# Reordering the hand-written instruction orders of a Mamba layer with a mixture of experts, five engines on one core

## The reference

```python
xz = layernorm(x) @ W_in + b_in                 # 128 -> 2 * 256
u, z = silu(xz[:, :256]), xz[:, 256:]
B, C = split(u @ W_xproj + b_xproj)             # 16 states each
dt = softplus(u @ W_dt + b_dt)
h_t = exp(dt_t * A) * h_{t-1} + dt_t * u_t * B_t   # per channel and state
y_t = sum_s h_t[s] * C_t[s] + D * u_t
x = x + (y * silu(z)) @ W_out + b_out
n = layernorm(x)
p = softmax(n @ gate_w.T); comb = p where among the top 2 of p + gate_bias, else 0
x = x + shared(n) + sum_e comb[:, e] * expert_e(n)   # 8 experts of width 256
# expert(n) = (silu(n @ w1.T) * (n @ w3.T)) @ w2.T
```

## Time and profile before

| | |
|---|---|
| median of 3 runs | 1292.01 us (1288.14 to 1292.46) |
| profiled execution, its own time | 1290.66 us |
| its span | 1288.5 us |
| busy PE / DVE / ACT / POOL | 1179.8 / 1174.2 / 1126.6 / 1112.8 us |
| TensorE clock granted, mean | 0.97 of full speed |
| DMA | 152.74 MB, 31.3% of 16 engines' time |

### The profile page before, as it was taken

One profiled execution on the slowest core, in us unless ns is written; L12 is line 12 of the kernel. 1 busy time (PEld: TensorE's weight loads), 2 busy tenths in 40 slices (PEclk: granted clock), 3 DMA queues, 4 the chain that ended last, 5 costly groups with the idle time before them and its releaser, 6 DMA issues.

```text
span 1288.5 us, 25674 instructions
## 1 busy us (share of the span) xinstructions
PE 1179.8 (92%) x7200; PEld 946.2 (73%) x7200; DVE 1174.2 (91%) x1833; ACT 1126.6 (87%) x1965; POOL 1112.8 (86%) x902
## 2 busy tenths in 40 slices
PE   4565899999999999999999999999999999999998
PEld 2334587877878787787778777777878778788887
DVE  1779899999999999999999999999999999999954
ACT  6674889999998999999899999989989998999854
POOL 2999899898999989899998989999898999998700
PEclk8776899999999999999999999999999999999999
DMA  8233331605234160523415052331505243250000
GB/s 305 121 146 125 133 148 39 250 1 207 82 132 155 54 232 0 205 81 137 150 62 225 0 205 81 144 142 67 220 0 210 77 152 135 71 208 9 10 9 9
DMA packets 47942, 152.74 MB, mean 119 GB/s; under 512 B 4512, under 2 KB 29472, under 8 KB 31392
## 3 DMA queue, kind: packets, MB, share of 16 engines
q1 hardware_dynamic: 47904, 152.28, 31.3%
HBM read 147.03 MB, written 5.24 MB: 118 GB/s over the span
## 4 chain that ended last, share of the span: by engine, by line
POOL 27%; issue 23%; PE 22%; DVE 19%; ACT 7%; DVEq 1%; DMA 0%; POOLq 0%; ACTq 0%; SPq 0%
POOL dbu L673 16%; PE h L938 10%; POOL hc L681 7%; DVE da L773 6%; PE mixed L907 5%; DVE hc L773 5%; PE y_acc L920 4%; POOL dt_s L661 3%; DVE g L815 2%; ACT L625 2%; ACT silu L625 2%; ACT da L589 1%; DVE acc L823 1%; DVE stats L743 1%; DVE hc L781 1%
## 5 line engine op out<-in xcount | busy, mean ns | idle before, releaser
L673 POOL TENSOR_TENSOR dbu<-w_s,b_all 128x512 f32<-128x512 f32 x512 | 650.3, 1289 | 5.7 <-DVE da L773 3.0
L681 POOL TENSOR_TENSOR hc<-hc,c_all 128x512 f32<-128x512 f32 x272 | 350.5, 1292 | 82.1 <-DVE hc L773 80.6
L589 ACT ACTIVATE da<-dt_s,a_neg 128x512 f32<-128x512 f32 x512 | 346.7, 692 | 84.2 <-DVE hc L781 70.0
L773 DVE TENSOR_TENSOR_SCAN hc<-da,dbu 128x512 f32<-128x512 f32 x272 | 328.1, 1211 | 12.0 <-PE y_acc L920 10.9
L920 PE MATMUL y_acc<-ident,hc 128*128 128x128 f32 x2048 | 295.0, 280 | 32.5 <-POOL hc L681 27.3
L773 DVE TENSOR_TENSOR_SCAN da<-da,dbu 128x512 f32<-128x512 f32 x240 | 292.6, 1219 | 27.4 <-ACT da L589 15.1
L920 PEld LDWEIGHTS y_acc<-ident,hc 128*128 128x128 f32 x2048 | 247.5, 144 | 81.5 <-POOL hc L681 36.2
L907 PE MATMUL mixed<-w_s,g 128*128 128x128 f32 x2304 | 283.4, 276 | 3.2 <-DVE g L815 1.2
L907 PEld LDWEIGHTS mixed<-w_s,g 128*128 128x128 f32 x2304 | 270.6, 192 | 15.4 <-DVE g L815 10.1
L938 PE MATMUL h<-x_hi,w_hi 128*128 128x512 f32 x576 | 264.1, 458 | 7.4 <-DVE g L815 2.9
L938 PE MATMUL h<-x_hi,w_lo 128*128 128x512 f32 x576 | 228.4, 396 | 0.0
(11 more groups left out here) (77 smaller groups left out, 1063.6 us busy)
## 6 DMA issues: line engine op xcount, KB each, us to landing
b_all<-bc_rows SPq DMA_DIRECT2D x64, 1024.0 KB, 4.7
c_all<-bc_rows SPq DMA_DIRECT2D x64, 1024.0 KB, 6.8
xt<-in_x SPq DMA_DIRECT2D x16, 256.0 KB, 6.5
res<-in_x SPq DMA_DIRECT2D x16, 256.0 KB, 6.9
out<-acc SPq DMA_DIRECT2D x16, 256.0 KB, 2.3
silu<-in_w SPq DMA_DIRECT2D x6, 256.0 KB, 4.1
w_s<-in_w SPq DMA_DIRECT2D x1, 1152.0 KB, 6.9
bc_rows<-bc_rows_s SPq DMA_DIRECT2D x16, 64.0 KB, 1.6
```

What stands on the lines that cost most here:

```text
L589: act.activation(da[a % DA_SLOTS][:, :], dt_s[:, c, :], ACT.Exp, scale=a_neg[:, a:a + 1]).then_inc(decay_made, 1)
L673: pool.tensor_tensor(dbu[:, a % DBU_SLOTS, :], w_s[:, c, :], b_all[:, s, :], ALU.mult).then_inc(dbu_made, 1)
L681: pool.tensor_tensor(slot, slot, c_all[:, s, :], ALU.mult).then_inc(c_by_pool, 1)
L773: dve.tensor_tensor_scan(dst, ring[:, :], dbu[:, a % DBU_SLOTS, :], 0.0, ALU.mult, ALU.add).then_inc(scanned, 1)
```

## The change

Only the three texts of orders and the code that reads them are changed; each engine has the same tasks as before, with the same shapes, buffers and semaphores. `START_ORDER` now covers sequences 0 to 2, `ORDER` windows 3 to 13 (4 to 13 as the loop), `END_ORDER` the last two windows. `LEAD` is 2, `LAG` 3. The window is cut elsewhere: PE's begins with `red.20` of sequence n-1 instead of `red.0` of n.

```diff
@@ -42,124 +42,205 @@
 ORDER = {
     "pe": """
-        red.0 red.1 red.2 h1.11-2 h3.9-2 gy.1-1 h1.12-2 red.3 eo.4-2 red.4 proj.0-1 h3.10-2 red.5 h1.13-2
-        z.0 z.1 h1.14-2 h1.15-2 h3.11-2 red.6 red.7 h3.12-2 red.8 eo.5-2 red.9 h3.13-2 x_t.0+1 red.10
-        h1.16-2 h1.17-2 xp.0+1 xp.1+1 h3.14-2 red.11 eo.6-2 red.12 h3.15-2 red.13 dl.0+1 h3.16-2 red.14
-        red.15 bc.0+1 h3.17-2 split.0-1 red.16 red.17 eo.7-2 red.18 dl.1+1 red.19 red.20 h1.0-1 red.21
-        red.22 h1.1-1 h1.2-1 eo.8-2 h3.0-1 h3.1-1 route.0-1 h3.2-1 red.23 red.24 h1.3-1 red.25 red.26 h1.4-1
-        eo.0-1 red.27 h1.5-1 gy.0 h1.6-1 h3.3-1 h3.4-1 eo.1-1 h3.5-1 h1.7-1 h3.6-1 red.28 h1.8-1 red.29
-        eo.2-1 h3.7-1 h3.8-1 red.30 red.31 eo.3-1 h1.9-1 h1.10-1
+        red.20-1 eo.5-3 red.21-1 dl.0 dl.1 red.22-1 red.23-1 red.24-1 red.25-1 h3.13-3 h3.14-3 eo.6-3
+        h3.15-3 split.0-2 h3.16-3 red.26-1 h1.17-3 red.27-1 h3.17-3 red.28-1 red.29-1 eo.7-3 red.30-1 h1.0-2
+        h1.1-2 h3.0-2 red.31-1 route.0-2 eo.8-3 h3.1-2 h1.2-2 red.0 h1.3-2 h1.4-2 red.1 red.2 h1.5-2 h1.6-2
+        red.3 h3.2-2 red.4 h1.7-2 h1.8-2 gy.1-1 h3.3-2 eo.0-2 h3.4-2 red.5 red.6 eo.1-2 proj.0-1 h3.5-2
+        red.7 h1.9-2 red.8 h1.10-2 h1.11-2 z.0 h3.6-2 eo.2-2 red.9 z.1 red.10 h1.12-2 red.11 h3.7-2 h1.13-2
+        red.12 h3.8-2 h3.9-2 x_t.0+1 eo.3-2 red.13 red.14 red.15 eo.4-2 h3.10-2 h1.14-2 h1.15-2 red.16
+        red.17 xp.0+1 xp.1+1 h1.16-2 red.18 gy.0 h3.11-2 bc.0+1 red.19 h3.12-2
     """,
     "act": """
-        zs.0 zs.1 silu.14-2 silu.15-2 decay.11 decay.12 norm1.0+1 decay.13 sc.5-2 x_tc.0+1 decay.14 decay.15
-        silu.16-2 u.0+1 silu.17-2 u.1+1 decay.16 decay.17 sc.6-2 norm2.0-1 decay.18 decay.19 dlc.0+1 ycopy.0
-        bcc.0+1 decay.20 splitc.0-1 xhi.0-1 decay.21 skip.0+1 decay.22 sc.7-2 decay.23 dlc.1+1 decay.24
-        decay.25 silu.0-1 silu.1-1 silu.2-1 decay.26 decay.27 sc.8-2 softe.0+1 rexp.0-1 decay.28 decay.29
-        softl.0+1 silu.3-1 silu.4-1 silu.5-1 silu.6-1 decay.30 decay.31 sc.1-1 decay.0+1 decay.1+1 silu.7-1
-        silu.8-1 decay.2+1 sc.2-1 decay.3+1 ycopy.1 decay.4+1 sc.3-1 decay.5+1 silu.9-1 silu.10-1 silu.11-1
-        decay.6+1 decay.7+1 decay.8+1 sc.4-1 decay.9+1 decay.10+1 silu.12-1 silu.13-1
+        norm1.0 decay.10-1 decay.11-1 sc.1-3 decay.12-1 silu.9-3 silu.10-3 silu.11-3 zs.0-1 decay.13-1
+        sc.2-3 decay.14-1 decay.15-1 silu.12-3 silu.13-3 zs.1-1 decay.16-1 decay.17-1 x_tc.0 sc.3-3
+        decay.18-1 decay.19-1 ycopy.0-1 sc.4-3 decay.20-1 decay.21-1 u.0 silu.14-3 u.1 silu.15-3 silu.16-3
+        decay.22-1 decay.23-1 norm2.0-2 decay.24-1 bcc.0 sc.5-3 decay.25-1 decay.26-1 dlc.0 decay.27-1 dlc.1
+        softe.0 decay.28-1 decay.29-1 softl.0 decay.30-1 decay.31-1 sc.6-3 splitc.0-2 xhi.0-2 decay.0
+        decay.1 silu.17-3 sc.7-3 silu.0-2 silu.1-2 decay.2 rexp.0-2 decay.3 ycopy.1-1 skip.0 sc.8-3 decay.4
+        decay.5 silu.2-2 silu.3-2 silu.4-2 silu.5-2 silu.6-2 decay.6 decay.7 silu.7-2 silu.8-2 decay.8
+        decay.9
     """,
     "dve": """
-        gyc.1-1 scan.6 mul.6 scan.7 scan.8 mul.8 comb.4-2 projc.0-1 mom1.0+1 g.10-2 agg1.0+1 scan.9 scan.10
-        g.11-2 mul.10 nb1.0+1 g.12-2 scan.11 scan.12 mul.12 scan.13 comb.5-2 mom2.0-1 agg2.0-1 g.13-2
-        scan.14 mul.14 scan.15 nb2.0-1 g.14-2 scan.16 scan.17 mul.16 comb.6-2 scan.18 g.15-2 mul.18 scan.19
-        scan.20 xlo.0-1 mul.20 scan.21 scan.22 mul.22 scan.23 g.16-2 g.17-2 comb.7-2 scan.24 mul.24 scan.25
-        g.0-1 scan.26 routec.0-1 mul.26 scan.27 rank.0-1 g.1-1 rank.1-1 comb.8-2 rank.2-1 g.2-1 rank.3-1
-        rank.4-1 scan.28 rank.5-1 rank.6-1 mul.28 scan.29 comb.0-1 g.3-1 gyc.0 g.4-1 rank.7-1 scan.30
-        scan.31 g.5-1 scan.0+1 comb.1-1 mul.0+1 g.6-1 scan.1+1 g.7-1 scan.2+1 mul.2+1 scan.3+1 comb.2-1
-        g.8-1 scan.4+1 scan.5+1 comb.3-1 mul.4+1 g.9-1
+        scan.7-1 gyc.1-2 g.3-3 comb.0-3 scan.8-1 mul.8-1 scan.9-1 scan.10-1 mul.10-1 g.4-3 g.5-3 comb.1-3
+        projc.0-2 scan.11-1 scan.12-1 mom2.0-2 mul.12-1 g.6-3 scan.13-1 comb.2-3 scan.14-1 g.7-3 scan.15-1
+        mul.14-1 agg2.0-2 g.8-3 scan.16-1 g.9-3 mul.16-1 scan.17-1 scan.18-1 mul.18-1 scan.19-1 comb.3-3
+        comb.4-3 g.10-3 scan.20-1 mul.20-1 nb2.0-2 scan.21-1 gyc.0-1 g.11-3 scan.22-1 mul.22-1 scan.23-1
+        scan.24-1 mul.24-1 comb.5-3 scan.25-1 scan.26-1 g.12-3 mul.26-1 scan.27-1 g.13-3 scan.28-1 mom1.0+1
+        scan.29-1 mul.28-1 g.14-3 g.15-3 scan.30-1 scan.31-1 comb.6-3 g.16-3 scan.0 xlo.0-2 mul.0 g.17-3
+        agg1.0+1 scan.1 comb.7-3 routec.0-2 g.0-2 scan.2 rank.0-2 mul.2 rank.1-2 scan.3 g.1-2 comb.8-3
+        rank.2-2 scan.4 rank.3-2 mul.4 rank.4-2 nb1.0+1 rank.5-2 scan.5 rank.6-2 g.2-2 scan.6 rank.7-2 mul.6
     """,
     "pool": """
-        hcp.7 dbu.10 dbu.11 rs1.0+1 dbu.12 dbu.13 hcp.9 hcp.11 dbu.14 dbu.15 hcp.13 dbu.16 rs2.0-1 dbu.17
-        dbu.18 dbu.19 hcp.15 dbu.20 hcp.17 dbu.21 dbu.22 dbu.23 hcp.19 dbu.24 hcp.21 dbu.25 dbu.26 hcp.23
-        hcp.25 dbu.27 dbu.28 dbu.29 hcp.27 dbu.30 dt.0+1 dbu.31 w.0+1 hcp.29 dbu.0+1 hcp.30 hcp.31 dbu.1+1
-        dbu.2+1 dbu.3+1 dt.1+1 dbu.4+1 dbu.5+1 hcp.1+1 dbu.6+1 hcp.3+1 dbu.7+1 hcp.5+1 dbu.8+1 resb.0
-        dbu.9+1 w.1+1
+        dbu.0-1 hcp.30-2 dbu.1-1 hcp.31-2 dbu.2-1 dbu.3-1 dbu.4-1 hcp.1-1 hcp.3-1 rs1.0 dbu.5-1 dt.1-1
+        dbu.6-1 dbu.7-1 dbu.8-1 hcp.5-1 dbu.9-1 dbu.10-1 dbu.11-1 hcp.7-1 hcp.9-1 resb.0-2 dbu.12-1 dbu.13-1
+        dbu.14-1 w.1-1 hcp.11-1 dbu.15-1 dbu.16-1 hcp.13-1 dbu.17-1 dbu.18-1 hcp.15-1 dbu.19-1 dbu.20-1
+        dbu.21-1 hcp.17-1 rs2.0-2 dbu.22-1 dbu.23-1 hcp.19-1 dbu.24-1 hcp.21-1 dbu.25-1 dbu.26-1 hcp.23-1
+        dbu.27-1 dbu.28-1 hcp.25-1 dbu.29-1 dbu.30-1 hcp.27-1 dbu.31-1 dt.0 w.0 hcp.29-1
     """,
     "sp": """
-        load.0+1 rows.0+1 spread.0+1 spread.1+1 store.0-2 spread.2+1 spread.3+1 loadres.0
+        loadres.0-1 rows.0+1 load.0+2 spread.0+1 spread.1+1 spread.2+1 store.0-2 spread.3+1
     """,
 }
 
 START_ORDER = {
     "pe": """
-        x_t.0 xp.0 xp.1 bc.0 dl.0 dl.1 z.0 red.0 red.1 red.2 red.3 z.1 x_t.0+1 red.4 red.5 red.6 xp.0+1
...
+        x_t.0 xp.0 xp.1 z.0 bc.0 dl.0 dl.1 z.1 red.0 red.1 x_t.0+1 red.2 red.3 red.4 xp.0+1 red.5 red.6
+        xp.1+1 red.7 red.8 dl.0+1 red.9 red.10 red.11 bc.0+1 red.12 red.13 dl.1+1 red.14 red.15 red.16
+        red.17 red.18 red.19 red.20 red.21 red.22 red.23 red.24 gy.0 red.25 red.26 red.27 red.28 red.29
+        red.30 red.31 red.0+1 gy.1 red.1+1 proj.0 z.0+1 red.2+1 red.3+1 red.4+1 red.5+1 red.6+1 z.1+1
+        red.7+1 x_t.0+2 red.8+1 red.9+1 xp.0+2 red.10+1 xp.1+2 red.11+1 red.12+1 red.13+1 red.14+1 red.15+1
+        bc.0+2 gy.0+1 dl.0+2 red.16+1 red.17+1 red.18+1 dl.1+2 red.19+1 split.0 red.20+1 route.0 red.21+1
...
     """,
     "act": """
-        norm1.0 x_tc.0 u.0 u.1 bcc.0 whi.0 dlc.0 dlc.1 softe.0 softl.0 decay.0 zs.0 decay.1 norm1.0+1 skip.0
...
+        norm1.0 x_tc.0 u.0 u.1 zs.0 bcc.0 dlc.0 dlc.1 softe.0 softl.0 decay.0 decay.1 skip.0 whi.0 whi.1
+        zs.1 decay.2 whi.2 decay.3 norm1.0+1 decay.4 decay.5 decay.6 x_tc.0+1 decay.7 decay.8 decay.9
...
     """,
     "dve": """
-        mom1.0 agg1.0 nb1.0 mom1.0+1 agg1.0+1 nb1.0+1 scan.0 mul.0 scan.1 scan.2 scan.3 mul.2 scan.4 wlo.0
...
+        mom1.0 agg1.0 nb1.0 mom1.0+1 agg1.0+1 scan.0 mul.0 scan.1 scan.2 nb1.0+1 scan.3 mul.2 scan.4 mul.4
+        scan.5 scan.6 scan.7 mul.6 scan.8 mul.8 scan.9 scan.10 mul.10 wlo.0 wlo.1 mom1.0+2 scan.11 scan.12
+        mul.12 scan.13 scan.14 scan.15 wlo.2 mul.14 scan.16 agg1.0+2 mul.16 scan.17 scan.18 mul.18 scan.19
+        scan.20 mul.20 scan.21 scan.22 scan.23 mul.22 wlo.3 scan.24 wlo.4 wlo.5 mul.24 scan.25 scan.26
+        mul.26 scan.27 scan.28 mul.28 scan.29 gyc.0 scan.30 scan.31 wlo.6 scan.0+1 scan.1+1 mul.0+1 scan.2+1
+        nb1.0+2 mul.2+1 scan.3+1 scan.4+1 gyc.1 mul.4+1 scan.5+1 scan.6+1 mul.6+1 scan.7+1 projc.0 wlo.7
+        mom2.0 scan.8+1 mul.8+1 scan.9+1 agg2.0 scan.10+1 scan.11+1 wlo.8 mul.10+1 scan.12+1 scan.13+1
+        mul.12+1 scan.14+1 mul.14+1 nb2.0 scan.15+1 scan.16+1 mul.16+1 scan.17+1 scan.18+1 mul.18+1 gyc.0+1
+        scan.19+1 scan.20+1 mul.20+1 scan.21+1 scan.22+1 mul.22+1 scan.23+1 scan.24+1 mul.24+1 xlo.0
...
     """,
     "pool": """
-        rs1.0 resb.0 rs1.0+1 dt.0 dt.1 w.0 w.1 dbu.0 dbu.1 dbu.2 dbu.3 dbu.4 dbu.5 hcp.1 hcp.3 dbu.6 dbu.7
...
+        rs1.0 rs1.0+1 resb.0 dt.0 dt.1 w.0 w.1 dbu.0 dbu.1 dbu.2 dbu.3 dbu.4 hcp.1 dbu.5 dbu.6 hcp.3 dbu.7
...
     """,
     "sp": """
-        load.0 loadres.0 rows.0 load.0+1 spread.0 spread.1 spread.2 spread.3 rows.0+1 spread.0+1 spread.1+1
-        spread.2+1 spread.3+1
+        load.0 load.0+1 loadres.0 rows.0 spread.0 spread.1 spread.2 load.0+2 spread.3 rows.0+1 spread.0+1
+        spread.1+1 spread.2+1 spread.3+1 load.0+3 rows.0+2 spread.0+2 spread.1+2 spread.2+2 spread.3+2
+        loadres.0+1 rows.0+3 load.0+4 spread.0+3 spread.1+3 spread.2+3 spread.3+3 store.0
     """,
 }
 END_ORDER = {
     "pe": """
...
+        eo.5-4 red.20-2 red.21-2 dl.0-1 dl.1-1 red.22-2 red.23-2 red.24-2 h3.13-4 red.25-2 h3.14-4 h3.15-4
```

(58 more changed lines are left out.)

141 lines of the change are left out of this document (94 added, 47 removed).

## The result

The changed kernel takes **1312.11 us** (median of 4 runs, 1305.33 to 1321.28) where the kernel before, run beside it, took 1291.03 (1288.14 to 1292.46): a ratio of 1.017, 95% interval 1.010 to 1.025. It is slower, where 1283 was forecast, and outside the range. The profiled execution is the longest of the four (1321.28 us), so its rows show more of the trouble than the median has.

A forecast was written before the change was run, and what follows sets the result against it. No single engine was taken as the bound: four lie within 3.3 us per window, and order decides the brief waits. 1290.66 + 0.5 - 4.5 - 3.3 - 9 + 8.6 = 1283 us; range 1268 to 1303.

The forecast's parts named there:

- Costs used: All engines: fixed start-to-start costs per instruction, summed per window to DVE 71.1, PE 67.7, ACT 67.9, POOL 69.3 us before.
- The window: Repeated window, sequences 3 to 12: 73.9 us instead of 74.8 from more even orders, -9 us over ten windows.
- evenness over stretches of eight steps: Repeated window: average of the largest engine sum per eight-step stretch falls from 76.1 to 75.2 us; 1.2% taken as gain.
- Table loads: ACT: 14 per window instead of 13, 226 in all instead of 209; 1.28 us more per window, covered by idle time.
- Then it costs nothing: ACT's extra 1.28 us table load per window is free while ACT keeps its present 5.2 us of idle time.
- The start: Up to sequence 2: first `dt` chain about 1 us later, counted +0.5; sequence 1 -4.5 us, sequence 2 -3.3 us.
- the -3.3: Sequence 2: 71.5 us instead of 74.8, with sums DVE 63.1, PE 62.2, ACT 62.3, POOL 69.3.
- The end: Sequences 13 to 15 and after: FFN work comes back, +0.5, +4.7, +0.9 and +2.5, together +8.6 us.
- Tail: FFN behind the last `red`: PE has 60.4 us for 57.9, so +2.5 on 63.0 us.
- The slower one: Rival, chance 0.22: in each window `res` reloads too late and POOL's `resb` waits; 1307 us.
- The tight window: Rival, chance 0.18: the window tightens to DVE's busy time, 72.7 us, -21 instead of -9; 1271 us.
- nothing comes of it: Rival, chance 0.18: buffers already absorb uneven stretches, so evenness gives nothing; edges leave +1.3, 1292 us.

The follow-up runs named there:

- experiment 1: Changed kernel with `var + eps` written as a sum by tensor_reduce instead of tensor_scalar: 1296.14 us, ratio 1.0045.
- experiment 2: Kernel before with `var + eps` written as a sum by tensor_reduce instead of tensor_scalar: 1280.32 us, ratio 0.992.
- second edit: The ranking's all-pairs comparison reads one operand from PSUM, on top of tensor_reduce for `var + eps`: 1276.00 us in the old order, 1301.59 in the new.
- experiments 11 and 8: `var + eps` by tensor_reduce and one operand of the ranking's comparison from PSUM: 11 in the changed kernel, 1301.59 us; 8 in the kernel before, 1276.00 us.
- experiment 3: Kernel before with `softl` two decays earlier in the repeated window, one more table load per window: 1294.22 us, ratio 1.0025.
- Experiment 6: Kernel before with tensor_reduce for `var + eps` and six of each sequence's 36 `h1` and `h3` computed twice on PE: 1339.99 us, ratio 1.038.
- lock-free: Either kernel with `var + eps` by tensor_reduce instead of tensor_scalar: changed kernel 1296.14 us, kernel before 1280.32 us.
- Experiments 9 and 10: Kernel before with tensor_reduce for `var + eps` and 10.5 us of PE work doubled: 9 in the start, 1285.33 us; 10 at the end, 1290.51 us.

## Why the prediction was wrong, by its steps

Forecast and profiled span differ by 38.7 us (-7.7 and +31.0): 31.4 of them in the ten windows (-9 and +22.4), 3.7 up to sequence 2, 3.6 in the end. Of the windows' +22.4 the lock on `var + eps` makes 25.1, less the 6.8 that it cost the same windows before, and the new order +4.2.

The whole span splits in the same way: experiment 1 minus experiment 2 is the order without this lock, 1294.1 - 1278.4 = +15.7 us; the lock costs the changed kernel 1319.5 - 1294.1 = 25.4 and the kernel before 1288.5 - 1278.4 = 10.1. Together 15.7 + 25.4 - 10.1 = 31.0. In medians 15.8 + 16.0 - 10.6 = 21.2. The +15.7 is not the order's cost free of all locks: with the second edit in both kernels (experiments 11 and 8) the spans are 1301.6 and 1276.7, 24.9 apart.

**Costs used: failed.** I took each instruction to have one duration and made sums of an order from them. `var + eps` was in none of the rows I read; in my sums it was a trifle. Its time depends on where it stands beside POOL's text, so a new order changes a cost and not only waits. By the spans that is 15 us, half of the profiled difference; by the medians 5, a quarter.

**The window: failed.** 73.9 was forecast; 75.1 is the best and 77.1 the mean of the ten. Without the lock it is 74.5 against 74.1 of the old order: evenness over stretches of eight steps gained nothing, although the sums fell by 1.2%. DVE is busy for 1.1 us less there (70.74 for 71.88 us), but now it waits for ACT, in the window from 547.87 of experiment 1 (total us, times, longest):

```profile
DVE da L870 <- ACT da L682: 2.6, 3, 1.4
```

Before, that was 0.3. Each of the three scans waits for a `decay` that stands right behind a table load (at 556.16, 579.86 and 594.37), and none of these loads is the new one behind `softl` (at 609.80). So the 0.23 us per window of experiment 3, 2.3 of the ten windows' +4.2, can't simply be carried over; no run tested where the loads stand in the new order. This step was the bulk of the forecast, and nothing of before had shown that evenness over such stretches is worth anything.

**Table loads: count right, price wrong.** "Then it costs nothing" was 0.23 us per window in the old order. An engine's idle time, summed over a window, covers a load only where that idle time lies. The Trainium skill (ScalarE: Activation LUTs, "Table sets: the hidden batching unit") has exp and ln in one set. The trace doesn't agree: a load of 1.28 us stands between `softl` and the next `decay` in the new order too (at 609.80 in experiment 1), and 17 more loads were run in all.

**The start: half right.** The first `dt` comes at 26.96 for 26.40, as forecast. From `hcp.31` of sequence 0 to that of 1 it is 70.4 us for 70.5 forecast, but the first of them ends 3.1 us later than before (102.02 for 98.93), so by this mark only 1.5 us are gained up to the end of sequence 1; the copies of `y_acc` have +1.0 and 68.4 for 73.8. Sequence 2 has 75.5, 73.9 without the lock, for 71.5: the -3.3 did not come. It is nearly as full as any other window (PE 68.7, DVE 69.9, ACT 67.8, POOL 70.4 us busy of 73.9), only with a largest sum of 69.3, and I let the largest sum stand for the time. Experiment 6 shows what that misses.

**The end: mechanism right, size wrong**, +12.2 for +8.6 (lock-free +15.1). The two stretches that carry it, sequence 13 and 14 of experiment 1:

```profile
994.71:1073.94 79.23, 76.45 (x470) 60.90 (x470) 76.75 (x121) 75.03 (x134) 71.80 (x60) 1.00 0.32 121
1073.94:1155.85 81.91, 81.35 (x519) 68.04 (x518) 76.53 (x116) 77.11 (x135) 68.47 (x55) 1.00 0.29 105
```

Against 74.1 each in experiment 2 that is +5.1 and +7.8 for forecasts of +0.5 and +4.7. In sequence 13 PE is busy for 4.7 us more than in experiment 2 (71.74) and the time grows by 5.1; I had let PE's 72.5 vanish under a window of 74.8 that it did not set. DVE and ACT are busy for 4.9 and 5.6 us more there, so that it is PE that sets this time is not shown; in sequence 14, where PE is busy for 81.35 of 81.91 us, it is. Tail: +1.9 for +2.5, right. PE's busy time moved is 10.7 + 3.1 us out of sequences 1 and 2, and 4.7 + 9.6 + 0.1 + 2.0 into the end. Experiments 9 and 10 give these 47% and 97%: about -6.5 and +16; measured -4.7 (-3.5 with the later start chain) and +15.1. That this comes so near is in part luck: the start's price is loose, and the change moved DVE and ACT work along with PE's.

**Rivals.** The slower one had the right sign and nearly the size (1307), by the wrong mechanism: `res` lands in 2.8 us at the median (6.9 before), as it must for the forecast, and POOL waits for it once, 0.3 us. The tight window and "nothing comes of it" are both refuted; the latter came nearest on the lock-free window. No rival had an instruction whose duration depends on the order, and that is what was missing from the list.

## What to carry to other kernels

Before sums are made from durations, look at the min, median and max of every small VectorE instruction: one that takes 0.17 us here and 1.3 there waits for GpSimd while it is counted as busy, and the lists of waits don't have it. Take the dependence away first (a reduction, or one operand in PSUM; 15 us here in the kernel before, with no new order), then reorder, and measure each step: the second edit gained 4.3 us in one order and lost 5.5 in the other. Sums of fixed costs can't see any of this. And where four engines lie within 5% of each other, the one with the largest sum does not set the time alone: PE work put into the windows cost 85% of its time, while a table load on ACT cost 18% of its own. So move work to where its engine is really idle, and pay attention to where the loop's phase leaves it at the end.

## What the runs showed of the hardware that was not expected

A VectorE instruction that needs what GpSimd holds waits for the end of GpSimd's instruction, and where GpSimd goes straight on it may miss that end: waits of 0.94, 2.3 and 3.43 us were one, two and three ends of instructions of 1.25 us each. Windows of one text, with VectorE level to 0.01 us and GpSimd's `dbu` under way for the same 0.36 us when the instruction starts, went either way (0.94 at 592.48, 3.43 at 899.45); what decides is open. Where GpSimd's next instruction waited for this very result (kernel before, 1.05 us) no second miss was seen. The changed kernel's runs spread over 16 us, those of experiment 1, without this wait, over 2.3.

TensorE's granted clock was 0.98 in three of the six bad windows and 1.00 in all other repeated ones: after TensorE had waited 2.3 us, it fell to 0.50 (1.2 GHz) three times and stayed at 1.00 three times. It plays no part in the repeated windows without the lock, which have 1.00 in both orders. A table load took 1.28 us everywhere, and in all but two cases each of the kernel before and the changed one the activation behind it started 0.01 us after its end.
